# Attention over eight batches: the batch loop written out, and a row-maximum product placed between score tiles

## What is computed

```
x = x + attn(layernorm(x))
x = x + ffn(layernorm(x))

attn: q, k = split(x @ W_qk + b_qk)     # 8 heads of 64, q and k interleaved
      v    = x @ W_v + b_v
      o    = softmax(q @ k^T / 8) @ v
      y    = layernorm(o @ W_out + b_out) * gamma + beta
      return (y + x) / sqrt(2)
ffn:  xr, xk = mixes of x with x one token earlier
      return sigmoid(xr @ W_r^T) * (square(relu(xk @ W_k^T)) @ W_v^T)
```

## Time and profile before

| what | value |
|---|---|
| median of three runs | 2773.16 us |
| the profiled execution, its time | 2776.32 us |
| span of its trace | 2774.5 us |
| TensorE busy | 95% |
| VectorE, ScalarE, GpSimd busy | 61%, 47%, 51% |
| mean granted TensorE clock | 0.988 |

### The profile page before, as it was taken

How to read it: one execution, slowest core, us unless ns; L and a number is a source line. 1 busy time by engine, 2 the same in 40 slices (tenths; PEclk the granted TensorE clock), 3 DMA queues, 4 the chain that set the end, 5 groups by cost and what they waited for, 6 DMA issues and landing times. The chain is left out here.

```text
span 2774.5 us, 36018 instructions
## 1 busy us (share of the span) xinstructions
PE 2641.1 (95%) x11376; PEld 1784.3 (64%) x11376; DVE 1685.7 (61%) x2691; ACT 1295.2 (47%) x1789; POOL 1422.0 (51%) x755
## 2 busy tenths in 40 slices
PE   5999999999999999999999999999589999999999
PEld 4655656665565665666566556655367777777777
DVE  5555455555545544654554555454488888888885
ACT  2345245434534533453453354344365555555554
POOL 2475466557647655664674566567323332332333
PEclk9999999999999999999999999999799999999999
DMA  3111021121112112111111211122211111212110
GB/s 106 54 39 43 24 74 43 31 65 36 43 27 66 43 35 62 43 35 50 51 40 31 62 47 31 31 47 61 87 58 65 68 68 65 71 63 73 60 61 31
DMA packets 89739, 145.06 MB, mean 52 GB/s; under 512 B 20096, under 2 KB 20608, under 8 KB 89600
## 3 DMA queue, kind: packets, MB, share of 16 engines
q1 hardware_dynamic: 89600, 143.19, 18.0%
HBM read 75.24 MB, written 33.81 MB: 39 GB/s over the span
## 5 line engine op out<-in xcount | busy, mean ns | idle before, releaser
L403 DVE TENSOR_REDUCE half_max<-ps_max 128x1 f32<-128x512 f32 x1024 | 680.1, 687 | 552.9 <-PE ps_max L743 545.3
L314 POOL TENSOR_TENSOR acc<-acc,probs 128x1024 f32<-128x1024 f32 x384 | 913.7, 2379 | 148.2 <-ACT probs L593 119.8
L593 ACT ACTIVATE probs<-ps_st 128x1024 f32<-128x1024 f32 x512 | 521.7, 1023 | 600.6 <-PE ps_st L764 576.1
L775 PE MATMUL ps_o<-probs,v 128*64 128x512 f32 x2048 | 471.1, 602 | 14.3 <-issue 14.3
L310 POOL TENSOR_TENSOR acc<-probs 128x1024 f32<-128x1024 f32 x64 | 153.2, 2394 | 619.3 <-ACT probs L593 619.3
L763 PE MATMUL ps_st<-qA,kA 128*128 128x512 f32 x1024 | 414.9, 405 | 14.6 <-DMA qB<-max_row 9.4
L764 PE MATMUL ps_st<-qB,kB 65*128 65x512 f32 x1024 | 407.6, 398 | 0.0
L743 PE MATMUL ps_max<-kA,qA 128*128 128x512 f32 x1024 | 387.2, 417 | 10.9 <-DVE half_max L403 4.4
L775 PEld LDWEIGHTS ps_o<-probs,v 128*64 128x64 f32 x2048 | 136.7, 137 | 282.5 <-issue 257.7
L743 PEld LDWEIGHTS ps_max<-kA,qA 128*128 128x128 f32 x1024 | 189.1, 189 | 145.6 <-issue 69.3
L763 PEld LDWEIGHTS ps_st<-qA,kA 128*128 128x128 f32 x1024 | 194.5, 190 | 83.2 <-ACT probs L593 33.7
(11 more groups left out here) (172 smaller groups left out, 4481.3 us busy)
## 6 DMA issues: line engine op xcount, KB each, us to landing
stage<-in_L_attn_x_dram SPq DMA_DIRECT2D x32, 512.0 KB, 6.0
qA<-qA SPq DMA_DIRECT2D x128, 128.0 KB, 2.2
kB<-kA SPq DMA_DIRECT2D x128, 128.0 KB, 2.3
o_scratch<-oT SPq DMA_DIRECT2D x128, 128.0 KB, 2.3
stage<-o_scratch SPq DMA_DIRECT2D x16, 1024.0 KB, 5.6
xc<-in_L_attn_x_dram SPq DMA_DIRECT2D x16, 1024.0 KB, 5.3
out_dram<-gate SPq DMA_DIRECT2D x64, 256.0 KB, 2.0
inv_cols<-inv_scratch SPq DMA_DIRECT2D x126, 128.0 KB, 2.8
```

The costliest lines, as they stand in the source:

```text
L314: pool.tensor_tensor(acc[:, :], acc[:, :], probs[:, j, :], ALU.add).then_inc(acc_done, 1)
L403: dve.tensor_reduce(half_max[:, r, kh:kh + 1], ps_max[(j + 1) % 2][:, :], AX_X, ALU.max).then_inc(max_done, 1)
L593: act.activation(probs[:, j, :], ps_st[j % 2][:, :], ACT.Exp).then_inc(exp_done, 1)
L775: ins = pe.matmul(ps_o[half * DH:(half + 1) * DH, :], v[:, j, hd * DH:(hd + 1) * DH], probs[:, j, half * HALF:(half + 1) * HALF], start=(j ...
```

## The change

The hardware loop over b becomes a Python loop on all five engines, so that its seven rounds are written out one after the other with constants in every wait and address. In `plain_head` row 5 moves behind score tile 2, and row 7 behind the first four matmuls of the projection; in `late_v_head` row 5 moves behind score tile 2. The number of matmuls and of all other operations stays.

```
-                with sp.Fori(0, B - 1) as b:
+                for b in range(B - 1):
                     for h in range(2, HEADS + 2):
                         head(b, h, False)
...
-                with pool.Fori(0, B - 1) as b:
+                for b in range(B - 1):
...
-                    dve.tensor_copy(ln1_stats[:, bass.ds(b * TT, TT), 0], mean_var[:, :, 0])
-                    dve.tensor_copy(ln1_stats[:, bass.ds(b * TT, TT), 1], rstd[:, :]).then_inc(stats_kept, 1)
+                    dve.tensor_copy(ln1_stats[:, slice(b * TT, b * TT + TT), 0], mean_var[:, :, 0])
+                    dve.tensor_copy(ln1_stats[:, slice(b * TT, b * TT + TT), 1], rstd[:, :]).then_inc(stats_kept, 1)
...
-                with dve.Fori(0, B - 1) as b:
+                for b in range(B - 1):
...
-                with act.Fori(0, B - 1) as b:
+                for b in range(B - 1):
...
@@ plain_head (TensorE)
                     scores(b, h, 0, 1)
                     rows(b, h + 1, 3, 4)
-                    scores(b, h, 1, 3)
-                    rows(b, h + 1, 4, 6)
+                    scores(b, h, 1, 2)
+                    rows(b, h + 1, 4, 5)
+                    scores(b, h, 2, 3)
+                    rows(b, h + 1, 5, 6)
                     scores(b, h, 3, 4)
-                    rows(b, h + 1, 6, 8)
+                    rows(b, h + 1, 6, 7)
                     more = not (last and h == HEADS - 2)
                     if more:
                         free_of_qk(b, h + 1, 1)
                         project_qk(b, h + 2, 0, 0, 4)
+                    rows(b, h + 1, 7, 8)
                     scores(b, h, 4, 5)
@@ late_v_head (TensorE)
                     rows(b, h + 1, 3, 4)
-                    scores(b, h, 1, 3)
-                    rows(b, h + 1, 4, 6)
+                    scores(b, h, 1, 2)
+                    rows(b, h + 1, 4, 5)
+                    scores(b, h, 2, 3)
+                    rows(b, h + 1, 5, 6)
                     scores(b, h, 3, 4)
                     rows(b, h + 1, 6, 7)
...
-                with pe.Fori(0, B - 1) as b:
+                for b in range(B - 1):
```

More of the change, by code:

```diff
@@ L548, in keep_stats @@
                     act.wait_ge(rstd_done, b + 1)
-                    act.activation(ln1_stats[:, bass.ds(b * TT, TT), 0], mean_var[:, :, 0], ACT.Copy)
-                    act.activation(ln1_stats[:, bass.ds(b * TT, TT), 1], rstd[:, :], ACT.Copy).then_inc(stats_kept, 1)
+                    act.activation(ln1_stats[:, slice(b * TT, b * TT + TT), 0], mean_var[:, :, 0], ACT.Copy)
+                    act.activation(ln1_stats[:, slice(b * TT, b * TT + TT), 1], rstd[:, :], ACT.Copy).then_inc(stats_kept, 1)
                 def normalise(b, t):
```

## The result

The changed kernel takes 2752.88 us (median of four runs, 2752.77 to 2753.57), beside 2773.8 us for the kernel before (four runs, 2770.03 to 2775.39): a ratio of 0.9927, with a 95% interval from 0.9910 to 0.9944. The profiled execution took 2752.77 us with a span of 2751.0 us, 23.5 us less than the span of before.

The account below looks back on a forecast made before the run. TensorE's order and small waits were taken to set a head's time, GpSimd's chain next as floor. Branches 18.1 plus order 1.8 gave 19.9 us, 2776.3 - 19.9 = 2756.4; 2755 us was taken, range 2747 to 2760.

Parts of the forecast that it names:

- part 1: TensorE at six loop branches: idle pieces and half clock behind them go with written-out code, 18.1 us, bounds 14.7 and 18.1.
- the other engines' branches cost nothing: Branches of engines other than TensorE: they have slack there, hidden by TensorE's matmuls, costed at nothing.
- part 2: Rows 4 and 5 around score tiles: wait moves from ScalarE's exponent to VectorE's chain, gain nothing, bounds 0 and 0.31 us a head.
- part 3: Row 7 behind four projection matmuls: TensorE gains 0.17 us a head, 0.24 in place 5, 7.0 us on TensorE alone.
- Row 9, on the edge: TensorE's row 9 waits for row 7's reduction, done about 1.15 us after row 7 starts; load due at 1.17, just in time.
- part 4: GpSimd's additions with constants: no plain head under 25.94 us, so the order brings 1.8 of TensorE's 7.0 us.
- TensorE keeps its whole gain: Rival, plain heads: GpSimd's chain isn't the floor, sum 25.1 us, 2751.2 against the profiled time or 2748 against the median; chance 0.15.
- the load 0.12 us behind the last addition: Sign for GpSimd's floor: line 785's load for the column sums always starts 0.12 us after its last addition.
- the 1.04 us from load to next head: End of a plain head: next head opens 1.04 us after line 785's load, giving the floor 24.90 + 1.04 = 25.94 us.
- 1.8 us on top: Row order's gain under GpSimd's floor: 33 heads about 1.1 us, 7 of place 5 0.7 us, beside the branches' 18.1.
- place 6 keeps its length: Places 0, 6 and 7 have over 2 us between last addition and line 785's load, so their length stays.
- the 3.2 us between the profiled execution of before and its median: Profiled execution lay 3.2 us above the median of three runs; the forecast median is 2753.3 or 2756.4, by the difference's kind.

Follow-up runs that it names:

- the swapped waits: Changed kernel with the two waits ahead of each of GpSimd's last six additions in the other order, previous addition first, then exponent; 2746.09 us, ratio 0.9909.
- A longer chain: Changed kernel with one 128 x 256 memset on GpSimd ahead of the fourth addition of each head; 2762.39 us in one run.
- a shorter chain: Changed kernel with GpSimd's last addition of a head cut to 128 of 1024 columns; 2741.15 us in one run.
- either way to the short spacing: Changed kernel with the additions' two waits swapped, 2746.09 us, or with GpSimd alone keeping its batch loop, 2745.83 us.
- the order alone: Kernel before with its loops kept and only the order of rows 4 to 7 changed; 2767.86 us, ratio 0.9985.
- the reduction placed between: Changed kernel, waits swapped (also GpSimd's first addition), VectorE's row 3 reduction between low parts of keys and queries, plain heads and place 0; 2734.99 us, ratio 0.9873.

## Why the prediction was right

The forecast of 2755 us with a range of 2747 to 2760 holds the 2752.88 measured. The mechanism is right for the branches, the rows and GpSimd's floor. That the heads' total came so close to the sum is in part luck: terms of 0.5 to 1.8 us that the sum didn't have, in both directions, nearly cancel there (below).

**The branches** (part 1) are right in kind and size. The row of 14.3 us is gone, no half clock is left from 72 to 1914 us, and the six heads across a branch lost 17.9 us, where 18.1 was the sum. By the Trainium skill's rule ("Runtime: NRT & Kernel Launch", Instruction fetch mechanics) a taken branch to a place outside the window waits for its page, and crossing a block in straight code is mostly hidden. The traces agree for TensorE in what they can show: six idle pieces of 2.03 to 2.60 us at the branches, none in the written-out code. That these pieces are the fetch of a page, no run here shows. That the other engines' branches cost nothing was right only as long as TensorE's own stood in front of them: alone, they cost about 0.9 us a round.

**Rows 4 and 5** (part 2): tile 3 was to stay at 7.71 and stands at 7.73. The reason, VectorE's chain, was tested by taking it away: then row 5 is free and tile 3 comes 0.2 us earlier.

**Row 7** (part 3): 0.17 us a head on TensorE were forecast. The new order's loops show 0.16, the swapped waits 0.14 to 0.16. Row 9, on the edge in the forecast, isn't held.

**GpSimd's floor** (part 4): 25.94 us was forecast for all plain heads, and they are 25.93 to 25.99, most of them 25.95 to 25.97: the chain ends 24.82 us into the head (416.53 - 391.71), not 24.78. A longer chain moves the floor by its own length. With a shorter chain, or with either way to the short spacing, the heads fall to TensorE's own 25.81 to 25.85. The rival "TensorE keeps its whole gain" fell, but not by the time: it had 0.15 and 2748 to 2751.2 us, and 2752.88 lies as near to that as to 2755. It fell by the heads, and by its reason: every head with constants has the long spacing, wherever it stands. With the waits swapped its outcome comes true, at 2746.09. One sign of mine was too weak: the load 0.12 us behind the last addition shows also where GpSimd isn't the floor, and the 1.04 us from load to next head is what tells.

**What was off.** The order was to bring 1.8 us on top, 1.1 in 33 heads and 0.7 in place 5; against the kernel that is only written out it brings 0.9 in the heads. Against the kernel before, the heads of places 1 to 4 that cross no branch gained about 0.1 us together, apart from the one pause below, and not 1.1. I took the loop's heads for comparison, and the 0.7 us of place 5 come with writing out: there the kernel only written out has 25.98 to 26.00 too, where the loop had 26.07. I said that place 6 keeps its length; its seven heads took 29.59 to 29.65 us before and take 29.36 to 29.40, 1.8 us in all. It does the same with TensorE alone written out and doesn't with the order alone, so it belongs to TensorE's own list. The register instructions ahead of its waits may be the cause, but no run took these alone. Against it stand pauses that I had priced at nothing. The head from 365.41 to 391.71 us is 0.33 us too long, and GpSimd's timeline shows where:

```profile
372.71 2.39 POOL L310 TENSOR_TENSOR acc<-probs 128x1024 f32<-128x1024 f32 x1 [7.22 <-ACT probs L593]
375.55 15.01 POOL L314 TENSOR_TENSOR acc<-acc,probs 128x1024 f32<-128x1024 f32 x6 [0.45 <-ACT probs L593]
```

The first of the six additions starts 0.3 us late although its inputs are there. A second plain head is longer by 0.3 in the same way, at the fourth of the six, and one of place 7 by 0.35, where the row of maxima is late: 1.0 us over the pass. A fetch of instructions would be a guess; with the waits swapped such pauses are absent from the plain heads, so what they hang on stays open. The last plain head, too, is 0.5 us longer than before (26.41 us, 25.89 before, 25.91 in the kernel only written out). TensorE had idled 2.09 us in it for the last addition, and the granted clock fell to half at 1914.5 us, 1.2 us before the last head opens:

```profile
1914.50:1915.70 1.20, 1.20 (x5) 0.05 (x1) 0.00 (x0) 0.00 (x0) 0.70 (x1) 0.52 0.00 0
```

The 3.4 us that went before head 1, with the clock, and 1.0 us behind the attention pass were in no term of the sum. So the heads gained 17.9 us at the branches (one of the three pauses lies in such a head and is counted there), 1.8 in place 6 and 0.8 in place 5. They lost 0.7 by the other two pauses, 0.5 by the clock and 0.1 here and there. That makes 19.1, near the 19.9 of the sum, by terms that offset each other. By the medians the gain is 20.9 us, by the two profiled executions 23.5; the range had room for this, since it allowed for the 3.2 us between the profiled execution of before and its median.

## What to carry to other kernels

When a loop is written out, compare how each engine's chain runs with constants and with registers; the chain of an engine with half its time idle can be the floor of every round, and heads already written out show it ahead of time. Where an instruction on GpSimd waits for two constant values, put the wait that ends early last in the program and look in the trace whether the instructions have moved together; with values in registers the original order had the short spacing, and other engines weren't tried. And before a product is moved out of a stall, see whether the two waits behind it end later than the one that is avoided.

## What the runs showed that I had not expected

- Two waits in either order differ by 0.06 us an addition on GpSimd with constants (six additions 14.99 against 14.65 us), and this decided about 5 us of the kernel.
- An idle piece isn't always followed by a fall of the clock. In the kernel before and in the one with the order alone, TensorE idled at twelve branches; the clock fell to half at the four pieces of 2.50 to 2.60 us and not at the eight of 2.03 to 2.48 us. But in the last plain head it fell at a piece of 2.09 us in the changed kernel and one of 2.12 us with TensorE alone written out, and not at one of 2.11 us in the kernel only written out. So the length of the piece alone doesn't decide.
- The spread of the runs was 5.4 us before (2770.03 to 2775.39) and 0.8 us in the changed kernel (2752.77 to 2753.57). The missing branches don't explain this: with the reduction placed between, also without a branch, four runs spread over 5.7 us (2732.45 to 2738.15).
- On TensorE a weight load that is released late costs 0.10 us more than its lateness: the matmul behind a held one comes 0.34 us later and not 0.23 (397.73 to 398.07, 399.11 to 399.44).
